# Laying out convolution filters before and during the first group: VectorE's part moved to ScalarE and GpSimd, in a two-convolution kernel

## The reference

```
x = x + conv31x31(gn(x), weight) + bias
x = x + conv11x11(gn(x), kernels(weight_coord, radius, weights))
```

## Time and profile before

| | |
|---|---|
| median of 3 runs | 3655.08 (3654.16 to 3655.74) |
| profiled execution, its own time | 3653.14 |
| span of its profile | 3651.4 |
| mean granted TensorE clock | 0.993 |
| busy share | PE 97%, DVE 92%, ACT 32%, POOL 1% |
| first matmul | 56.09 |
| DMA | 536.20 MB, mean 147 GB/s |

### The profile page before, as it was taken

How to read it: one execution, slowest core, us unless ns; L and a number is a source line. 1 busy time by engine, 2 the same in 40 slices (tenths; PEclk the granted TensorE clock), 3 DMA queues, 4 the chain that set the end, 5 groups by cost and what they waited for, 6 DMA issues and landing times.

```text
span 3651.4 us, 60133 instructions
## 1 busy us (share of the span) xinstructions
PE 3543.0 (97%) x19008; PEld 3343.8 (92%) x19008; DVE 3370.9 (92%) x5113; ACT 1185.6 (32%) x1234; POOL 26.2 (1%) x9
## 2 busy tenths in 40 slices
PE   3799999999999999999999999999999999999996
PEld 3699999999999999999999999999999999999995
DVE  7889999999999999999999999999999999999987
ACT  2223333333333333333333333333333333333332
POOL 2000000000000000000000000000000000000000
PEclk9899999999999999999999999999999999999998
DMA  6977677787678777678777678777778776778653
GB/s 138 200 138 149 139 145 157 151 152 152 138 144 158 150 153 153 136 145 158 156 147 152 139 146 159 156 149 147 144 147 159 155 149 141 148 149 159 127 108 82
DMA packets 809792, 536.20 MB, mean 147 GB/s; under 512 B 464475, under 2 KB 771803, under 8 KB 809243
## 3 DMA queue, kind: packets, MB, share of 16 engines
q1 hardware_dynamic: 809626, 534.73, 74.3%
...
## 4 chain that ended last, share of the span: by engine, by line
PE 94%; DVE 1%; SPq 1%; issue 0%; DMA 0%; ACT 0%; DVEq 0%
PE acc L909 94%; SPq L399 1%; DMA toep<-padded 0%; DVE y_image L704 0%; DVE yt L694 0%; DVE xt L670 0%; DVE xt L677 0%; SPq L409 0%; DVE x_lo L684 0%; ACT x_hi L528 0%; DVE halves L624 0%; DVE norm L654 0%; DVE raw L712 0%; DVE part L661 0%; DVE halves_tmp L630 0%
## 5 line engine op out<-in xcount | busy, mean ns | idle before, releaser
L909 PE MATMUL acc<-x_hi,toep 128*112 128x448 f32 (+3 forms) x12672 | 3385.3, 348 | 97.7 <-DVE x_lo L684 67.2
L909 PEld LDWEIGHTS acc<-x_hi,toep 128*112 128x112 f32 x12672 | 2263.5, 181 | 232.1 <-issue 87.0
L909 PE MATMUL acc<-x_lo,toep 128*112 128x448 f32 (+3 forms) x6336 | 2211.0, 349 | 0.0
L909 PEld LDWEIGHTS acc<-x_lo,toep 128*112 128x112 f32 x6336 | 1143.4, 180 | 64.5
L528 ACT ACTIVATE x_hi<-xt 128x1440 fp32r<-128x1440 f32 x384 | 541.2, 1409 | 1800.2 <-DVE xt L677 1800.2
L684 DVE TENSOR_TENSOR x_lo<-xt,x_hi 128x1440 fp32r<-128x1440 f32 x384 | 629.1, 1638 | 75.8 <-ACT x_hi L528 74.7
L694 DVE TENSOR_TENSOR yt<-acc,p 128x896 f32<-128x896 f32 x384 | 415.8, 1083 | 66.9 <-PE acc L909 57.6
L520 ACT ACTIVATE images<-raw,norm 128x896 f32 (+1 forms) x384 | 439.6, 1145 | 49.8 <-DVE norm L654 49.8
L661 DVE BATCH_NORM_STATS2 part<-raw 96x6 f32 (+3 forms) x768 | 449.1, 614 | 1.3
L677 DVE TENSOR_TENSOR xt<-xt 128x960 f32<-128x960 f32 x384 | 442.3, 1152 | 7.9
L670 DVE STREAM_TRANSPOSE xt<-images 128x960 f32<-128x960 f32 x384 | 444.7, 1158 | 2.9 <-ACT images L520 1.4
...
...
## 6 DMA issues: line engine op xcount, KB each, us to landing
...
raw<-in_x_dram SPq DMA_DIRECT2D x96, 672.0 KB, 10.5
out_dram<-raw SPq DMA_DIRECT2D x192, 336.0 KB, 5.0
...
```

Of the source, the lines that this page charges most:

```text
L909: last = nc.tensor.matmul(dst, toeplitz(toep, f, place, part, k), src[:, h, cols], start=(m == matrices[0][0] and part == 0 and src is x_h ...
```

## The change

- The filters' three stages have another order: channels 0 to 95 of the 31x31 filter before the loop, then the 11x11 filters (jobs 1 and 2), then channels 96 to 191 of the 31x31 filter (jobs 4 and 5). Each has its own place in the ring. Only the margins of the padded areas and the entries that no tap reaches are zeroed, no whole areas.
- ScalarE's own DMA queue loads the weights of channels 0 to 95 and three small parameters. SyncE loads x of group 0 in three parts of two channels, with a semaphore each, then the later weights and the bias. VectorE takes statistics part by part.
- The stores and the loads of x in the loop move: the first stage's last half at job 1, x of group 1 at job 2, the 11x11 filters' store at 3, their first matrices at 4, the last stage's store at 5 (a third) and 6 (two thirds), x of group 2 at 7. The store at 5 waits for all of the last stage. Statistics of group 2 in iteration 1 are taken later.
- In every normalisation seven small copies become four; it has 22 counted instructions.

```diff
-NORM_STEPS = 25
+NORM_STEPS = 22
...
-MEASURED_SECOND_GROUP = {2: [0, 1], 4: [2, 3], 6: [4, 5]}
+MEASURED_SECOND_GROUP = {6: [0, 1, 2], 8: [3, 4, 5]}
...
+        AREAS = [[0, f1.padded],
+                 [2 * f1.padded + K1 * K1 + k * f2.padded for k in range(4)],
+                 [CG * RUN, CG * RUN + f1.padded]]
+        W1_FIRST = 2 * f1.padded
+        WORK_START = [W1_FIRST + K1 * K1, AREAS[1][3] + f2.padded, CG * RUN + 2 * f1.padded]
+        WORKS = [2, 2, 1]
+        w1_first = spare[:, W1_FIRST:W1_FIRST + K1 * K1]
+
+        STAGES = [[(f1, 0, 0), (f1, 0, 1)],
+                  [(f2, 0, 0), (f2, 0, 1), (f2, 1, 0), (f2, 1, 1)],
+                  [(f1, 1, 0), (f1, 1, 1)]]
+        BEFORE = [0, 2, 6, 8]
...
-        STAGES = [[(f1, 0, 0)], [(f1, 1, 0)], [(f2, 0, 0), (f2, 1, 2)]]
...
-            sp.dma_start(w1_src, weight1.rearrange("(t p) o h w -> p t (o h w)", p=CP)).then_inc(w_landed, 16)
-            load_x(0)
-            sp.dma_start(w2_src[:], weight2.rearrange("o (t p) n -> p t (o n)", p=CP)).then_inc(params_landed, 16)
-            sp.dma_start(coord_all[:], coord.rearrange("o n e -> o (n e)").to_broadcast([CP, POINTS * 2])).then_inc(params_landed, 16)
-            sp.dma_start(radius_all[:], radius.rearrange("o n a b -> o (n a b)").to_broadcast([CP, POINTS])).then_inc(params_landed, 16)
-            sp.dma_start(bias_all[:], bias.rearrange("(o c) -> o c", o=1).to_broadcast([P, C])).then_inc(params_landed, 16)
+            for c in range(0, CG, 2):
+                for q in range(BANDS):
+                    sp.dma_start(raw_band(0, q, c, c + 2), dram_band(x_dram, 0, q, c, c + 2)).then_inc(x0_landed[c // 2], 16)
+            sp.dma_start(w1_later[:], weight1[CP:2 * CP].rearrange("p o h w -> p (o h w)")).then_inc(w_later_landed, 16)
+            sp.dma_start(bias_all[:], bias.rearrange("(o c) -> o c", o=1).to_broadcast([P, C])).then_inc(bias_landed, 16)
...
             store_filters(0, 0, CG)
-            sp.wait_ge(padded_stored, 16 * 2)
-            sp.wait_ge(toep_zeroed, 2)
+            filters_stored()
+            sp.wait_ge(toep_zeroed, 1)
             for m in range(T_RING):
                 load_toeplitz1(m, m)
-            store_filters(0, CG, CP)
+            store_filters(0, CG, CP // 2)
 
             def filters_and_first_loads(k):
 
+                if k == 1:
+                    store_filters(0, CP // 2, CP)
                 if k == 2:
+                    filters_stored()
+                    load_x(1)
+                if k == 3:
                     store_filters(1)
-                if k == 3:
-                    sp.wait_ge(padded_stored, 16 * STORED[1])
-                    sp.wait_ge(x_landed, 16 * BANDS)
-                    load_x(1)
                 if k == 4:
-                    store_filters(2)
-                if k == 5:
-                    sp.wait_ge(padded_stored, 16 * STORED[2])
+                    filters_stored()
+                    sp.wait_ge(toep_zeroed, 2)
                     for m in range(T_RING):
                         load_toeplitz2(m, m)
-                    sp.wait_ge(x_landed, 16 * BANDS * 2)
+                if k == 5:
+                    store_filters(2, 0, CP // 3)
+                if k == 6:
+                    store_filters(2, CP // 3, CP)
+                if k == 7:
+                    filters_stored()
+                    sp.wait_ge(x_landed, 16 * BANDS)
                     load_x(2)
...
-            nc.gpsimd.memset(area[:, area_size // 2:], 0.0).then_inc(area_zeroed, 1)
-            pool.wait_ge(area_zeroed, 1)
...
+            def taps_11x11():
+
+                for k in range(K2):
+                    at = -1.0 + 2.0 * k / (K2 - 1)
+                    nc.gpsimd.memset(lin[:, 0, k:k + 1], at)
+                    step(nc.gpsimd.memset(lin[:, 1, K2 - 1 - k:K2 - k], at))
+                pool.wait_ge(radius_inverted, 1)
+                for p in range(POINTS):
+                    for axis in range(2):
...
+            def filters_low(k):
+
+                for u, (f, t, e) in enumerate(STAGES[k]):
+                    done = BEFORE[k] + u
+                    pool.wait_ge(taps_laid, 2 * (done + 1))
+                    pair = work(k, u).rearrange("p k o (m s) -> p k o s m", s=2)
+                    for o in range(2):
+                        nc.gpsimd.tensor_tensor(work_sums(k, u)[:, :, o, :], pair[:, :, o, 0, :], pair[:, :, o, 1, :],
+                                                ALU.add).then_inc(sums_ready, 1)
+                    pool.wait_ge(sums_ready, 2 * (done + 1))
+                    low, high = padded_rows(k, u, 1).bitcast(F32R), padded_rows(k, u, 0)
+                    pool.wait_ge(w_hi_ready, 2 * done + 1)
+                    nc.gpsimd.tensor_tensor(low[:, :, :, 0:f.D], work(k, u), high[:, :, :, 0:f.D], ALU.subtract
+                                            ).then_inc(w_lo_ready, 1)
+                    pool.wait_ge(w_hi_ready, 2 * done + 2)
+                    nc.gpsimd.tensor_tensor(low[:, :, :, f.D:f.L], work_sums(k, u), high[:, :, :, f.D:f.L], ALU.subtract
+                                            ).then_inc(w_lo_ready, 1)
+                    pool.wait_ge(w_lo_ready, 2 * (done + 1))
+                    if WORKS[k] == 1 and u == 0:
+                        for x in untapped(k, 1):
+                            nc.gpsimd.memset(x, 0.0).then_inc(untapped_cleared, 1)
+                        pool.wait_ge(untapped_cleared, len(untapped(k, 1)))
+
...
             nc.gpsimd.memset(toep1[:].bitcast(F32), 0.0).then_inc(toep_zeroed, 1)
+            pool.wait_ge(toep_zeroed, 1)
+            zero_last_band(0, 1)
+            pool.wait_ge(last_band_zeroed, 1)
+            taps_11x11()
+            pool.wait_ge(w_lo_ready, 2 * BEFORE[1])
+            clear(1, area2_zeroed)
             nc.gpsimd.memset(toep2[:].bitcast(F32), 0.0).then_inc(toep_zeroed, 1)
             pool.wait_ge(toep_zeroed, 2)
-            zero_last_band(0, 1)
-            pool.wait_ge(last_band_zeroed, 1)
+            filters_low(1)
             zero_last_band(1, X_RING)
             pool.wait_ge(last_band_zeroed, 2)
+            pool.wait_ge(padded_stored, 16 * 10)
+            clear(2, area1_zeroed)
+            filters_low(2)
...
+            def lay_taps(k, u):
+
+                f, t, e = STAGES[k][u]
+                if u >= WORKS[k]:
+                    act.wait_ge(w_lo_ready, 2 * (BEFORE[k] + u - WORKS[k] + 1))
+                source = (taps2[:, t, :] if f is f2 else w1_later[:] if t else w1_first)
+                taps = source.rearrange("p (h w) -> p h w", w=f.K)
+                for o in range(2):
+                    column, first, count = f.taps(e, o)
+                    nc.scalar.activation(work(k, u)[:, :, o, first:first + count],
+                                         taps[:, ::-1, column:column + 2 * count - 1:2], ACT.Copy).then_inc(taps_laid, 1)
...
+            act.dma_start(w1_first, weight1[0:CP].rearrange("p o h w -> p (o h w)")).then_inc(w_landed, 16)
+            act.dma_start(w2_src[:], weight2.rearrange("o (t p) n -> p t (o n)", p=CP)).then_inc(params_landed, 16)
+            act.dma_start(coord_all[:], coord.rearrange("o n e -> o (n e)").to_broadcast([CP, POINTS * 2])).then_inc(params_landed, 16)
+            act.dma_start(radius_all[:], radius.rearrange("o n a b -> o (n a b)").to_broadcast([CP, POINTS])).then_inc(params_landed, 16)
+            act.wait_ge(w_landed, 16)
+            act.wait_ge(bufs_zeroed, BUFS_ZEROED)
+            lay_taps(0, 0)
+            lay_taps(0, 1)
+            high_taps(0, 0)
+            high_sums(0, 0)
+            high_taps(0, 1)
+            high_sums(0, 1)
             root(0)
             act.wait_ge(last_band_zeroed, 1)
             for s in slots(0)[:AHEAD]:
                 normalise(0, s)
                 high(0, s)
             normalise(*later(0, 0, AHEAD))
-            act.wait_ge(params_landed, 16 * 4)
+            act.wait_ge(bias_landed, 16)
+
+            def filter_share(n):
+
+                if n == 1:
+                    act.wait_ge(area2_zeroed, 1)
+                    for u in range(2):
+                        lay_taps(1, u)
+                    for u in range(2):
+                        high_taps(1, u)
+                        high_sums(1, u)
+                if n == 2:
+                    for u in range(2, 4):
+                        lay_taps(1, u)
+                    for u in range(2, 4):
+                        high_taps(1, u)
+                        high_sums(1, u)
+                if n == 4:
+                    act.wait_ge(area1_zeroed, 1)
+                    act.wait_ge(w_later_landed, 16)
+                    lay_taps(2, 0)
+                    high_taps(2, 0)
+                    high_sums(2, 0)
+                if n == 5:
+                    lay_taps(2, 1)
+                    high_taps(2, 1)
+                    high_sums(2, 1)
...
-                    if peeled and i == 0 and job(i, s) in (0, 2):
```

(27 more changed lines are left out.)

217 lines of the change are left out of this document (111 added, 106 removed).

## The result

The changed kernel takes **3621.57 us** (median of 4 runs, 3621.23 to 3621.92) against 3654.62 for the kernel before on the same chip (3653.55 to 3655.74): 33.1 us less, a ratio of 0.9909 with a 95% interval of 0.9897 to 0.9921. Forecast were 3624 and a gain of 30.9.

A forecast was written before the change was run, and what follows sets the result against it. TensorE bounds the kernel (busy 3543.0 of 3651.4 us), so only time before 200 us can be won: 18 from the earlier start plus 13 from gaps and restarts, 30.9 in all, giving 3624 us, range 3609 to 3641.

The forecast's parts named there:

- First matmul at 38: Before the loop: filters ready at 18.4, statistics to 24.8, normalisation to 31.2, then 6.9; 18 us earlier, range 35 to 44.
- The removed wait: Before the loop: VectorE's two layout copies took 9.71 us behind GpSimd's Toeplitz memset, against 0.85 for a later pair.
- "x in three parts" and "parameters: 0": Before the loop: x's last part is there when first statistics finish; parameters on ScalarE's own queue cost 0.
- PSUM memset and taps: 0: Before the loop: PSUM memset fits the weights' wait; 11x11 taps moved to GpSimd cost 0, covered by ScalarE's slack.
- Job 4's gap 4.0: In the loop: x of group 1 queued ahead of job 4's matrices, landed 96.8; gap 4.0 plus 1.6 restart.
- SyncE free at 131: In the loop: SyncE waits for later filters until 131, stores a third; job 7's matrices land 144.9, gap 6.6.
- Job 10's gap 1.4: In the loop: job 10's matrices, queued behind x of group 2, land at 179.5; gap 1.4, restart 1.6.
- Restarts at 1.6 each: In the loop: each TensorE gap costs 1.6 us beyond its length, because the granted clock is lower around gaps.
- No gap at all: Rival, in the loop: queue drains at the steady pace, no gap after the start; gain 48.7, 3606.4 us; chance 0.12.
- GpSimd at its far price: Rival: GpSimd needs 10.5 us a filter, SyncE held 9 more, 6 lost before the loop; gain 16, 3639; chance 0.22.
- SyncE held at job 5: Slower rival: at 17 us a filter on GpSimd, ScalarE is late too; 44 lost against 31, 3668; chance 0.05.
- Start given back: Rival: weights or parameters land late beside x, later gaps take the rest; gain 0 to 8, 3651; chance 0.05.

The follow-up runs named there:

- e12_taps_after_norm: The changed kernel with GpSimd's 11x11 taps begun only when the first normalisation is done: 3620.30 us, ratio 0.9905.
- e5_seven_copies: The changed kernel with the seven small copies of each normalisation again in place of four: 3620.87 us, ratio 0.9909.
- e4_before_memset_later: The kernel before, with GpSimd's memset of the Toeplitz ring held until the first 31x31 filters are laid out: 3650.85 us, ratio 0.999.
- e7_before_no_lock: The kernel before, with GpSimd's Toeplitz memset held until filters are laid out and its later band memset until the first channel is normalised: 3644.82 us, ratio 0.9973.
- e6_x_whole: The changed kernel with x of group 0 in four DMAs of 672 KB instead of twelve of 224 KB: 3625.44 us, ratio 0.9921.
- e10_x_whole_late_recip: The changed kernel with x of group 0 in four whole DMAs and VectorE's parameter wait and reciprocal moved behind the low parts: 3621.16 us, ratio 0.9908.
- e2_x1_at_3: The changed kernel with x of group 1 loaded at job 3, behind job 4's matrices, in place of job 2: 3626.05 us, ratio 0.9923.
- e3_split_and_6: The changed kernel with the last filter stage stored whole at job 6 and x of group 1 split around job 4's matrices: 3618.94 us, ratio 0.9902.
- e13_both_shares_job3: The changed kernel with both of ScalarE's shares of the last filter stage at job 3, stores unchanged: 3610.89 us, ratio 0.9879.
- e9_shares_earlier: The changed kernel with the last filter stage stored whole at job 6 and ScalarE's two shares of it at jobs 3 and 4: 3611.67 us, ratio 0.9883.

## Why the prediction was right, and where it was not

**Right in its mechanism**: fewer idle microseconds at the start and in the ramp, the same pace afterwards. That job 7 starts within 0.2 us of the forecast is luck, as shown below. Its point of comparison was the start of job 12, 30.9 us earlier; job 11's output shows 33.5. The steps:

- **First matmul at 38, measured 35.28.** The filters were ready at 16.71 instead of 18.4. Three terms were too dear: the table load (1.28) fell into the wait for the weights, the four layout copies took 0.58 us each and not 0.75 (0.7 in all), and the microsecond for waiting on GpSimd was not needed. Against them went a later begin, 6.58 instead of 6.1, and small waits. The normalisation took 5.1 us (23.09 to 28.18) instead of 6.4: I had put 2 us for its copies behind GpSimd, and `e12_taps_after_norm` shows 0.55 for everything from the last low part to the first matmul. The 0.5 for fewer copies is 0.3 by their own rows, and nothing in the start (`e5_seven_copies`).
- **The removed wait.** The 9.71 us were put down to the memset, and `e4_before_memset_later` and `e7_before_no_lock` show it. The Trainium skill's rule (SBUF — State Buffer, Who interferes with whom) holds for copies as small as 32 x 2 too, in these runs. Its second half, that two-input VectorE work is held up by a GpSimd read, the trace also bears out: before the loop for little, 1.30 against 1.16 at L842; in the loop for more, 2.83 and 2.53 at the same line while GpSimd does its low parts. The first of these ends 1.0 us after GpSimd's 2.89 us instruction, and GpSimd's next ends 1.4 after it, so each stands for a large part of the other. The forecast priced only GpSimd's standing behind VectorE, not this.
- **"x in three parts" and "parameters: 0".** The forecast had x there in time whole or split, and that is so. That the parameters have a queue of their own and cost nothing is true only beside small transfers: with x whole they cost 4 to 5 us at the start (`e6_x_whole`, `e10_x_whole_late_recip`). The number was right, the reason wrong.
- **PSUM memset and taps: 0.** Right. The memset is in the wait for the weights. The taps take GpSimd 30 us (12.3 to 42.3) in place of VectorE's 11, and ScalarE did not wait for them (its areas' first copies stand at 58.70, 0.72 us for four).
- **Job 4's gap 4.0, measured 4.24.** Right. `e2_x1_at_3` and `e3_split_and_6` show that it can't be had by changing the order alone. It stands at 4.31 in the fastest version; whether earlier issue of the matrices of jobs 1 to 3 would shorten it was not tried.
- **SyncE free at 131, measured 129.7; job 7's matrices at 144.9, measured 145.09.** The agreement is luck: two errors cancel. Job 3 ended at 89.15 (93.39 less 4.24) and not at 92.8, 2.7 us of that from the start and 0.9 because jobs 0 to 3 took 53.9 us and not 54.8. But from job 3's end to SyncE's release I had 38.2 us, measured are 40.6. Of these 2.4, 0.9 lie ahead of ScalarE's second share (VectorE's 2.83 at L842 stands there) and 1.5 behind it: the four rows of a filter take GpSimd 6.6 us and not 5.6, 7.5 with its wait for ScalarE. And from the release to job 7's start I had 13.9, measured are 15.4. So the 3.65 us won by job 3 were used up by 2.4 and 1.5 that I had priced too low, and job 7's gap is 10.04 instead of 6.6. They were not lost in a hold that has a clock of its own: in `e6_x_whole`, whose first matmul is 5.0 us later, the store and job 7 are 6.2 and 6.0 later, and in `e10_x_whole_late_recip`, 1.1 later, they are both 2.4 later. **By these runs everything up to job 7 moves with the start; without the extra 2.7 us job 7 would have started later than forecast.**
- **Job 10's gap 1.4 and its restart 1.6: not there.** This is the step that failed. From job 7's start to job 12's I had 55.5 us, 5.6 above the pace of 49.9 (three jobs of 13.3 and two of 5.0): 1.6 for job 7's restart, 3.0 for job 10, 1.0 for small waits. By the output rows, less the 0.8 us by which job 11's stood behind the start I read before, it was 52.7, 2.8 above the pace. That difference, 2.8, less the 0.2 at job 7, is the 2.6 between 30.9 and 33.5. I had job 10's matrices landed 1.4 us late, at the end of a queue priced at the 202 GB/s of the earlier trace rows for matrices and x; just ahead of it, from 145 to 149 us, the changed kernel moved 387 GB/s. Job 10 also came later than I had it: its output stands at 192.58, so with 13.3 us for its matmuls it started near 179.3 instead of 178.1, since job 7's restart cost 2.7 us and not 1.6. Matrices landed at the forecast's 179.5 would have made it wait 0.2 us, not 1.4. How much of the rest the faster queue did is not tested.
- **Restarts at 1.6 each.** They were not alike. Stretches of the changed kernel after its two long gaps:

```profile
93.00:97.00 4.00, 3.60 (x11) 3.12 (x12) 4.00 (x9) 0.00 (x0) 0.00 (x0) 0.57 1.08 313
97.00:101.00 4.00, 4.00 (x24) 3.84 (x23) 3.64 (x14) 0.00 (x0) 2.81 (x5) 1.00 1.14 189
145.00:149.00 4.00, 3.91 (x11) 3.34 (x12) 0.00 (x0) 0.00 (x0) 0.00 (x0) 0.50 0.96 387
149.00:152.00 3.00, 3.00 (x14) 2.83 (x13) 0.00 (x0) 0.00 (x0) 0.00 (x0) 0.65 1.15 210
152.00:156.00 4.00, 4.00 (x24) 3.83 (x23) 0.00 (x0) 1.68 (x2) 0.00 (x0) 1.00 1.18 220
```

  After 4.24 us of idling the granted clock is back at 1.00 by 97 us; after 10.04 us it stands at 0.50, the lower of the two levels (1.2 of 2.4 GHz), for four microseconds and is back only by 152. Jobs 4 and 5 took 27.7 us for 26.6, so that restart cost 1.2 us (by the unrounded rate); job 7's cost about 2.7 (23 matmuls from 145 to 152, 4.2 us of work at 0.1845, in 6.9). With it the 2.8 above the pace are accounted for, and no small waits are left.
- **Two slips in the sums.** The landing of 1.8 us is 1.7 by its own numbers (5.3 less 3.6), and the upper end of the range is 3641 where its terms add up to 3639. Neither touches the forecast.

**The rivals.** No gap at all (3606) is refuted in the changed kernel, yet `e13_both_shares_job3` comes within 4.5 us of it: most of what stood against it was the hold; job 4's gap of 4.31 us remains. GpSimd at its far price, and SyncE held at job 5 for good, did not come: no low part of the changed kernel on GpSimd is longer than 2.90. The Trainium skill's factor of about 2 for two-input work (GPSIMD Engine Reference, Performance versus the Vector engine) would have given 7.8 us a filter, an estimate; measured are 6.6 in the changed kernel against VectorE's 3.9, a factor of 1.7, and in `e9_shares_earlier` 2.87 against 1.98 for 96 x 992 and, with no VectorE work of two inputs beside it, 1.53 against 1.05 for 96 x 496, about 1.45 each. Start given back: no, 20.8 us came and the gaps shrank too.

**The ledger of the 33.1 us**, as far as the runs show it: 9.4 the lock (`e7_before_no_lock`); 11.4 the engines side by side and the memsets in the wait (read from traces); 12.7 the ramp (33.5 less the 20.8), from gaps of 14.9 instead of 22.2 and fewer slow restarts; less 1.6 from 200 us on. That is 31.9 of span; the medians say 1.2 more, within what the two series of runs scatter.
